# Sandwich block on one core: a prologue in which VectorE scales and halves the first group's tiles, GpSimd halves one overflow weight, and the second set of transposes goes to the projection's bank

## What is computed

```
g = sigmoid(xn @ Wg.T + bg);  h[t] = (1 - g[t]) * h[t-1] + g[t] * xn[t]     # along the 1024 tokens
x = x + layernorm(h @ Wo.T + bo)
eid = argmax(softmax(xn2 @ router_w + router_b))        # 8 experts, 320 places each, in order of tokens
y = relu(xn2 @ w1[eid] + b1[eid]) @ w2[eid] + b2[eid]   # for the tokens that found a place
y = relu(xn2 @ ow1 + ob1) @ ow2 + ob2                   # for all others: the overflow network
out = x + layernorm(y)
```

## Time and profile before

| | us |
|---|---|
| median of 3 runs | 1218.23 (1217.35 to 1219.71) |
| the profiled execution: its own time | 1216.73 |
| its span, first to last instruction | 1215.0 |
| PE busy | 1152.8 (95%) |
| DVE busy | 1012.0 (83%) |
| ACT busy | 733.8 (60%) |
| POOL busy | 726.4 (60%) |

### The profile page before, as it was taken

How to read it: one execution, slowest core, us unless ns; L and a number is a source line. 1 busy time by engine, 2 the same in 40 slices (tenths; PEclk the granted TensorE clock), 3 DMA queues, 4 the chain that set the end, 5 groups by cost and what they waited for, 6 DMA issues and landing times.

```text
span 1215.0 us, 24627 instructions
## 1 busy us (share of the span) xinstructions
PE 1152.8 (95%) x7657; PEld 1031.3 (85%) x7657; DVE 1012.0 (83%) x2758; ACT 733.8 (60%) x1296; POOL 726.4 (60%) x855
## 2 busy tenths in 40 slices
PE   5489999999999999999999999999999999899994
PEld 4378888888888888888888888888888888889994
DVE  4688888889888998889889888888889977678882
ACT  3256666656656665666666656556566666577772
POOL 4465656656666556565656666666565664256774
PEclk8799999999999999999999999999999999999997
DMA  8211111111111111111111011101111100344520
GB/s 252 87 43 38 53 49 46 41 37 35 35 35 35 35 35 35 35 35 35 35 35 35 18 34 35 35 20 32 35 35 35 35 18 18 109 144 155 175 87 27
DMA packets 59431, 65.06 MB, mean 54 GB/s; under 512 B 7835, under 2 KB 55629, under 8 KB 59268
## 3 DMA queue, kind: packets, MB, share of 16 engines
q1 hardware_dynamic: 52228, 59.32, 15.1%
q0 software_dynamic: 7168, 5.32, 1.5%
HBM read 40.17 MB, written 38.61 MB: 65 GB/s over the span
## 4 chain that ended last, share of the span: by engine, by line
PE 84%; DVE 5%; POOL 5%; issue 3%; ACT 2%; DMA 0%; DVEq 0%; POOLq 0%; ACTq 0%
PE psY L1122 11%; PE psY L1125 10%; PE psY L1124 10%; PE psH L1022 10%; PE psH L1024 10%; PE psH L1023 10%; PE psA L1022 5%; PE psA L1024 5%; PE psA L1023 5%; PE psT L1078 3%; POOL tok L410 2%; PE psT L1035 2%; DVE st L695 2%; POOL rstd L369 1%; PE psT L1084 1%
## 5 line engine op out<-in xcount | busy, mean ns | idle before, releaser
L369 POOL TENSOR_TENSOR rstd<-veps,mhalf 128x4 f32<-128x4 f32 (+1 forms) x144 | 195.6, 1358 | 386.6 <-DVE nmean L707 386.6
L536 ACT ACTIVATE hid<-psH,biasT 128x512 f32<-128x512 f32 (+2 forms) x320 | 206.3, 645 | 270.0 <-PE psH L1024 262.1
L1122 PE MATMUL psY<-W_hi,hid_hi 128*128 128x256 f32 x1200 | 347.4, 290 | 0.3 <-DVE hid_lo L841 0.3
L1125 PE MATMUL psY<-W_hi,hid_lo 128*128 128x256 f32 x1200 | 339.8, 283 | 0.0
L1124 PE MATMUL psY<-W_lo,hid_hi 128*128 128x256 f32 x1200 | 339.5, 283 | 0.0
L1022 PE MATMUL psH<-xfT_hi,W_hi 128*128 128x512 f32 (+2 forms) x640 | 241.6, 377 | 3.0 <-DVE xfT_lo L785 3.0
L1024 PE MATMUL psH<-xfT_hi,W_lo 128*128 128x512 f32 (+2 forms) x640 | 240.1, 375 | 0.0
L1023 PE MATMUL psH<-xfT_lo,W_hi 128*128 128x512 f32 (+2 forms) x640 | 239.9, 375 | 0.0
L841 DVE TENSOR_TENSOR hid_lo<-hid,hid_hi 128x512 fp32r<-128x512 f32 (+2 forms) x320 | 202.3, 645 | 42.8 <-ACT hid_hi L540 29.2
L1122 PEld LDWEIGHTS psY<-W_hi,hid_hi 128*128 128x128 f32 x1200 | 227.4, 189 | 9.8 <-DVE hid_lo L841 1.5
L1124 PEld LDWEIGHTS psY<-W_lo,hid_hi 128*128 128x128 f32 x1200 | 227.6, 190 | 6.6
(11 more groups left out here) (110 smaller groups left out, 2089.6 us busy)
## 6 DMA issues: line engine op xcount, KB each, us to landing
xin<-L_attn_x SPq DMA_DIRECT2D x32, 512.0 KB, 3.5
stage<-L_ffn_w SPq DMA_DIRECT2D x16, 1024.0 KB, 6.3
out<-outt SPq DMA_DIRECT2D x31, 512.0 KB, 2.9
xbuf<-zrow SPq DMA_DIRECT2D x1, 2570.0 KB, 18.1
xin<-xbuf SPq DMA_DIRECT2D x8, 257.0 KB, 5.7
stage<-L_ffn_ow SPq DMA_DIRECT2D x2, 1024.0 KB, 10.2
xbuf<-x,idx POOLq DMA_INDIRECT x128
b_b<-L_ffn_b SPq DMA_DIRECT2D x1, 1024.0 KB, 13.4
```

What stands on the lines that cost most here:

```text
L369: pool.tensor_tensor(rstd[k][:, t0:n], veps[k][:, t0:n], mhalf[:, t0:n], ALU.pow).then_inc(s_rs[k], 1)
L536: act.activation(hid[j % 2][:, at:n], psH[:, j % 2, at:n], ACT.Relu, bias=bias).then_inc(s_hid, 1)
L1122: pe.matmul(psY_t[:, t, :], hi, w[0][:, j, :], start=(j == 0 and t % 2 == 0), stop=False, skip_group_check=True)
L1125: last = pe.matmul(psY_t[:, t, :], lo_, w[0][:, j, :], start=False, stop=(j == HC - 1), skip_group_check=True)
```

## The change

It touches the prologue and one pair of waits in the first step.

- SP issues the loads of `ow2` and `ow1`, in that order and each with its own semaphore, right behind the load of x(0, 1), ahead of the broadcasts; before it issues the broadcast of `b2` it waits until both have landed.
- POOL keeps the small `deviation` pairs and the scalings of group (0, 1). The three sets of four scalings of group (0, 0) (`tok`, the one that ACT did in `norm1`, and `tok2`) go to DVE (`first_rows`), and so do both `state_lo` of the prologue. In return POOL does the two subtractions for `ow2`.
- DVE's own order is changed: `stats0((0, 1))` stands behind `xn_lo((0, 0))`; the recurrence of (0, 1) is cut in two halves, one before and one after `xf_lo`.
- ACT copies the first piece of `ow2` before the first sigmoid, and the second between the two `state_hi` copies.
- The second set of transposes of group (0, 0) goes to `psA`, and waits for `s_keep` of (0, 1) instead of `s_ngx`. The first `route`, which writes `psT`, now waits for `s_rw_lo` and for `s_ngx` of (0, 1).

```diff
@@ sync
             load((0, 1))
+            sp.dma_start(stage_w2(), ow2...).then_inc(s_w["ow2"], 16)
+            sp.dma_start(stage_w1(), ow1...).then_inc(s_w["ow1"], 16)
             for dst, src in ((bo_b[:], bo), (ob2_b[:], ob2), (rb_b[:], router_b)):
...
-            sp.dma_start(stage_w1(), ow1...).then_inc(s_w["ow"], 16)
-            sp.dma_start(stage_w2(), ow2...).then_inc(s_w["ow"], 16)
+            sp.wait_ge(s_w["ow2"], 16)
+            sp.wait_ge(s_w["ow1"], 16)
             sp.dma_start(b2_b[:], b2.partition_broadcast(P)).then_inc(s_w["b2"], 16)
@@ gpsimd
-            norm0((0, 0))
-            pool.wait_ge(s_tok, 1)
+            def overflow_w2_lo(q):
...
+                pool.wait_ge(s_ow_hi, q + 1)
+                pool.tensor_tensor(dst, stage[:, 1, cols], hi.bitcast(F32), ALU.subtract).then_inc(s_ow_lo, 1)
+
+            deviation(0, (0, 0), TG)
             norm0((0, 1))
-            state_lo((0, 0))
+            overflow_w2_lo(0)
+            overflow_w2_lo(1)
             deviation(1, (0, 0), TG)
-            norm2((0, 0), x1, TG)
-            state_lo((0, 1))
+            deviation(2, (0, 0), TG)
@@ scalar
             xn_hi((0, 0))
+            overflow_hi(1, 0)
             act.wait_ge(s_biasT, 2)
             sigmoid((0, 0))
-            state_hi((0, 0))
+            state_hi((0, 0), (0,))
+            overflow_hi(1, 1)
+            state_hi((0, 0), (1,))
+            xn_hi((0, 1))
...
-            norm1((0, 0))
+            overflow_hi(0, 0)
+            overflow_hi(0, 1)
             sigmoid((0, 1))
-            xf_hi((0, 0), GT)
+            xf_hi((0, 0), GT, turned=psA)
@@ vector
+            def first_rows(k, dst, src):
+                dve.wait_ge(s_nm[k], 1)
+                for t in range(TG):
+                    last = dve.tensor_scalar(dst[:, t, :], src[:, t, 0:D], rstd[k][:, t:t + 1], nmr[k][:, t:t + 1],
+                                             ALU.mult, ALU.add)
+                return last
...
@@ tensor, step
                     layer1(now, 0, GT, W1[1], at=sure(now) * P)
+                    if not live(grp(i, u, -1), NG):
+                        pe.wait_ge(s_rw_lo, 1)
+                        pe.wait_ge(s_ngx, cnt(nxt, 2, 2))
                     route(now)
@@ tensor, prologue
-            transposes1((0, 0), TG)
-            pe.wait_ge(s_rw_lo, 1)
+            pe.wait_ge(s_tok2, 1)
+            pe.wait_ge(s_keep, cnt((0, 1), 2, 2))
+            for c in range(DC):
+                for t in range(TG):
+                    last = pe.transpose(psA[:, c, t * P:(t + 1) * P], tok2[:, t, c * P:(c + 1) * P], ident[:])
+                last.then_inc(s_T1, 1)
             pe.wait_ge(s_ow_lo, 4)
```

More of the change, by code:

```diff
@@ L164, in sandwich_kernel @@
         s_xbuf0 = sem("s_xbuf0")
-        s_w = {n: sem(f"s_w_{n}") for n in ("wg", "wo", "rw", "ow", "bias", "bcast", "b2")}
+        s_w = {n: sem(f"s_w_{n}") for n in ("wg", "wo", "rw", "ow1", "ow2", "bias", "bcast", "b2")}
         s_const = sem("s_const")
@@ L259, in _ @@
             load((0, 1))
+            sp.dma_start(stage_w2(), ow2.rearrange("(c p) d -> p c d", p=P)).then_inc(s_w["ow2"], 16)
+            sp.dma_start(stage_w1(), ow1.rearrange("(c p) h -> p c h", p=P)).then_inc(s_w["ow1"], 16)
             for dst, src in ((bo_b[:], bo), (ob2_b[:], ob2), (rb_b[:], router_b)):
@@ L569, in sigmoid, with state_hi, xf_hi @@
                         .then_inc(s_keep, 1)
-            def state_hi(g):
+            def state_hi(g, cs=range(DC)):
                 i, v = g
                 act.wait_ge(s_wo, cnt(g, 2, 0))
-                for c in range(DC):
+                for c in cs:
                     act.wait_ge(s_scan, cnt(g, 2, c + 1))
                     act.activation(hst_hi[:, c, :], hst[v][:, c, :], ACT.Copy).then_inc(s_h_hi, 1)
-            def xf_hi(g, n, base=0):
+            def xf_hi(g, n, base=0, turned=psT):
                 act.wait_ge(s_l1, cnt(g, HC, 0) + HC * base)
@@ L631, in step, with overflow_hi @@
                     state_hi(far)
+            def overflow_hi(m, q):
+                dst = (W1, W2)[m][1][0][:].rearrange("p a b -> p (a b)")
+                act.wait_ge(s_w[("ow1", "ow2")[m]], 16)
+                act.activation(dst[:, q * 1024:(q + 1) * 1024], stage[:, m, q * 1024:(q + 1) * 1024], ACT.Copy)\
+                    .then_inc(s_ow_hi, 1)
             xn_hi((0, 0))
+            overflow_hi(1, 0)
             act.wait_ge(s_biasT, 2)
             sigmoid((0, 0))
-            state_hi((0, 0))
+            state_hi((0, 0), (0,))
+            overflow_hi(1, 1)
+            state_hi((0, 0), (1,))
+            xn_hi((0, 1))
             act.wait_ge(s_w["rw"], 16)
             act.activation(rw[:, :, 0:E], rw_raw[:], ACT.Copy).then_inc(s_rw_hi, 1)
[L639 to L645, removed]
-            norm1((0, 0))
+            overflow_hi(0, 0)
+            overflow_hi(0, 1)
             sigmoid((0, 1))
-            xf_hi((0, 0), GT)
+            xf_hi((0, 0), GT, turned=psA)
             state_hi((0, 1))
@@ L729, in xn_lo, with recurrence @@
                         .then_inc(s_xn_lo, 1)
-            def recurrence(g):
+            def recurrence(g, cs=range(DC)):
                 i, v = g
@@ L955, in _ @@
             stats1((0, 0))
-            overflow_lo(0)
+            overflow_w1_lo(0)
+            dve.wait_ge(s_att, 2)
+            first_rows(1, att, att).then_inc(s_u, 1)
             residual1((0, 0))
             stats2((0, 0))
-            recurrence((0, 1))
-            overflow_lo(1)
-            xf_lo((0, 0), GT)
+            overflow_w1_lo(1)
+            dve.wait_ge(s_x1, 1)
+            first_rows(2, tok2, x1[0]).then_inc(s_tok2, 1)
+            recurrence((0, 1), (0,))
+            xf_lo((0, 0), GT, turned=psA)
+            recurrence((0, 1), (1,))
+            dve.wait_ge(s_rw_hi, 1)
+            dve.tensor_tensor(rw[:, :, E:2 * E], rw_raw[:], rw[:, :, 0:E].bitcast(F32), ALU.subtract).then_inc(s_rw_lo, 1)
+            state_lo((0, 1))
             stats0((1, 0))
```

46 lines of the change are left out of this document (28 added, 18 removed).

## The result

| | before | changed |
|---|---|---|
| median, us | 1217.45 (1216.99 to 1220.01, 15 runs) | 1216.21 (1215.23 to 1217.51, 15 runs) |
| ratio | | 0.9984, 95% interval 0.9976 to 0.9992 |
| profiled execution: own time, span | 1216.73, 1215.0 | 1215.67, 1213.9 |
| PE, DVE, POOL busy | 1152.8, 1012.0, 726.4 | 1153.2, 1004.8, 709.1 |

The forecast was 1214.3, with a range of 1210.8 to 1217.5. Sign and range held; the size did not, and the time is that of rival B (1216.7), whose price the range had taken in. The prediction also gave 0.75 to a time under 1215.8, and that did not come.

What follows compares the result with a forecast made beforehand. PE is busy throughout 84 to 1000 us, so what reaches that stretch earlier ends earlier. Terms +0.15 - 0.95 - 3.9 + 0.6 + 0.2 = -3.9 gave a median of 1214.3, range 1210.8 to 1217.5.

Steps and rivals of the forecast that it cites:

- rival B: POOL's two ow2 subtractions get in twice among DVE's scan and halves; one more 128x1024, +2.4: 1216.7; chance 0.17.
- State of (0, 0): Prologue, up to project's start: one POOL 128x1024 subtraction gets in between DVE's last operations; project at 23.95, +0.15.
- rival B's second way: POOL's first subtraction comes before DVE's second scan, which precedes it by only 0.2 in the sum; +2.4.
- X: End of xn_lo((0, 0)) on DVE in the prologue: 13.69 before, forecast 12.5.
- base: Starting time of the sum: profiled execution 1216.73, giving 1212.8; it lies 1.5 under the median 1218.23, hence 1214.3.
- The scalings: Four 128x256 scalings on DVE, in three places of the prologue: 1.1 per set, range 0.65 to 1.4.
- norm 1: Group (0, 0), second set of scalings: ACT's 2.07 become DVE's 1.1, the deviation keeps its 2.3; -0.95.
- norm 2: Group (0, 0), end of nmean to end of tok2: 7.37 become 3.45 with the scalings on DVE; -3.9.
- Project and the statistics behind it: From project's start on PE to the end of norm 1's nmean: project itself unchanged, 0.
- route: First step on PE: route waits for the second ngx and rw_lo, 47.75 where 47.15 without the wait; +0.6.
- rival C: ACT waits for ow2's load; each microsecond of landing past 14.6 costs one; slower, about 1221; chance 0.03.
- rival D: PE's wait at 46.85 was for something behind the four scalings; no more than a gain of 1: 1217; chance 0.05.

Runs made afterwards that it cites:

- e9: Changed kernel with ow2's two subtractions on VectorE and norm 1's four scalings back on ScalarE: 1211.86 us, ratio to before 0.9945.
- e3: The changed kernel, unchanged, run and profiled a second time: 1216.50 us, ratio to before 0.9987.
- e7: Changed kernel with ow2's two subtractions on VectorE and norm 2's scalings (tok2) back on GpSimd: 1212.52 us, ratio to before 0.9956.
- e6: Changed kernel with ow2's two subtractions on VectorE and 28 unused identity transposes (fillers) on TensorE: 1211.43 us, ratio to before 0.9948.
- e11: Changed kernel, ow2's subtractions on VectorE, then ow1's on GpSimd behind a wait; 49 fillers, project (0, 0) before transposes (0, 1), xn of (0, 1) later: 1206.32 us.
- e5: Changed kernel with ow2's two subtractions on VectorE and ow1's two on GpSimd, without a wait between them: 1210.25 us, ratio to before 0.9933.
- e12: e11 with 64 more filler transposes, behind the gate of (0, 1) and before the first layer 1: 1209.58 us, ratio to before 0.9926.

## Why the prediction was right in sign and wrong in size

*State of (0, 0): this step failed.* "In one of those two gaps POOL gets in" was said of three DVE operations that stand against two of POOL. The pair got in twice in both profiles: in the first ahead of the scan and ahead of the halves, as rival B's second way has it; in the second ahead of each half, which neither of B's ways describes. What was wrong is not the exclusion but how often it bites. The sum priced one 128x1024 subtraction and put the second at nothing, where POOL had it queued and the two engines took turns: of three DVE operations in a row two are caught. Counted from X, which came at 12.90 and not at 12.5, POOL was ready at X + 6.84 (X + 6.8 in the sum) and project started at X + 13.74 (X + 11.45 in the sum): 2.29 more, one more subtraction, and 0.40 from X. The sum's order was scan first, by 0.15; the second profile has that order (scan at X + 6.57) and lost as much, so the margin decides which operation waits and not how many. Taking the pair away gives 5.15 us and a project at X + 9.59 (22.47), where the sum without an exclusion had X + 9.4. B had 0.17; it should have had more than the forecast. That the measured time lies in the range is not to the sum's credit: the range had B's price in it, and its base, the median of three runs (1218.23), was 0.78 above that of fifteen (1217.45). By the Trainium skill (SBUF — State Buffer, "SBUF: two separate sides") the lock is exclusive; the rows agree (a half that takes 0.68 by itself took 2.78 behind POOL's subtraction). How it goes when both engines have a next two-input operation ready is in no row of before, and the forecast rested on it.

*The scalings: mechanism right, size off.* 1.38 for four, in three places, where I took 1.1; 1.38 is next to the upper bound, the `bn_stats` of the same tile (1.40 in the earlier trace rows). That is 0.28 each, and explains norm 1 (-0.66) and norm 2 (-3.61) up to 0.03. The estimate of 0.9 from the Trainium skill's figure (VectorE: DVE Perf Modes, "The perf-mode tier table") is further off; the measurement decides.

*Project and the statistics behind it: +1.30 where I said 0.* The project itself took 0.85 more, at a granted clock of 0.50 where before had 0.63 in 23.8 to 28.4; before it PE had been idle for 5.54 instead of 1.86. That the longer wait made the clock slower is not shown: in e9 PE had been idle for 1.77 only and project took 5.45 at 0.50, and in e3 it took 4.89 at 0.58 after 4.93. Over the profiles without fillers it took 4.38 to 5.46, so this part is scatter that the sum had put at nothing. The other 0.45 lies in DVE's statistics ahead of the power (idle for 0.54 before `veps`, and for 0.53 in e3); its cause is open.

*Norm 1, norm 2, route: right.* Each is within 0.3, and e9 and e7 confirm two of them alone. The loop handed on what it got. The load of `ow2` cost nothing: ACT's first copy (12.07 to 13.12) was over long before `keep` at 16.07, so rival C is out; rival D is out with DVE's `tok` as the releaser at 46.75.

*The base.* One profile of before was taken for the kernel. It was a quick one; the second has layer 1 2.20 later, of which 0.78 come from the same exclusion and most of the rest from PE's pace in the gate and in project. Against the second one the changed kernel's layer 1 starts 2.3 and 3.1 earlier, against the first 0.1 and 0.9.

## What to carry to other kernels

Before an operation with two SBUF inputs goes to GpSimd, list what VectorE has to do in its whole length, and count the neighbours in the queue: two back to back can hold off VectorE twice. Work of this kind is cheap on VectorE in a stretch in which it waits anyway (2.35 against 4.76). If it goes to GpSimd, a wait that keeps it behind VectorE's cost less than the race in the one place where both were measured (second transposes at 40.29 against 41.21). When a term depends on which of two operations is first by 0.1 or 0.2 us, follow both orders to the end before pricing it, and take a second profile of the kernel before: one shows only one side. What a matrix engine gains in clock is only worth something if the next instruction in its own queue is the one that is ready (e6 against e11).

## What was not expected of the hardware

- DVE's scaling of 128x256 in 32 bits with two scalars of one value per partition: 1.38 for four, the pace of `bn_stats` (1.40).
- POOL's subtraction of 128x1024: 2.38 alone, up to 3.37 beside one of DVE. A power on 128x4: 1.01 alone, 1.91 to 1.92 beside a `W_lo` of DVE (1.22).
- The exclusion also holds a small single-input operation: in e11 DVE's `veps` (128x4) took 1.73, beside POOL's `W_lo`.
- Where both engines had their next two-input operation waiting, they took turns, the one whose row begins first going first: in both profiles of the changed kernel and in e5. The earlier trace rows differ: there `veps`, with one input, waited through both of POOL's.
- The gate's matmuls stand 0.43 apart in the changed kernel and 0.23 in e6, e11 and e12, while the granted clock of that stretch is 1.00 in all of them. With fillers ahead PE had been busy. Without them the pace changes from 0.43 to 0.23 inside the gate, after seven to ten of the twelve matmuls, or not at all, from one execution to the next (in the changed kernel's two profiles: not at all, and for the last three), and the second `keep` moves with it by up to 1.1. Project's matmuls of half the columns stand 0.21 apart at a granted clock of 0.50 and 0.12 at 1.00, so 0.43 is the pace of the lower clock; the profile's clock row does not show it there, and no run settled why.
